# Sources with several edges exchange first-layer sums by a packed list, the other rows stay in edge order, and the relational tiles run in one part

## The reference

```
L0: norm = rsqrt(1 + outdeg); agg[src] = sum of (norm*h)[dst]; x += norm * (agg + norm*h)
L1: w = -dis[src]*dis[dst]; four times feat[src] += sum of w*feat[dst]; x += polynomial(theta) of feat
L2: per edge: msg = sum_b w_comp[type, b] * (h[src] @ weight[b])
    a = tanh(relu(<h[src] A1, h[dst] A2 + rel_emb[type]> / sqrt(32)))
    x[dst] += relu(sum of a*msg over its edges + h[src of its last edge] @ self_loop)
L3: ten times h[dst] = 0.9 * norm * sum of (norm*h)[src] + 0.1 * h0;  x += h
```

## Time and profile before

| | us |
|---|---|
| median of 3 runs | 2677.03 (2675.88 to 2682.1) |
| profiled execution, span | 2683.2 |
| DVE busy | 1746.0 (65%) |
| POOL busy | 1681.8 (63%) |
| PE busy | 434.8 (16%) |
| ACT busy | 341.4 (13%) |
| DMA moved | 84.14 MB, mean 31 GB/s |

### The profile page before, as it was taken

The page is one execution under the profiler, slowest core; times in us unless marked ns, Lnnn a source line. Parts: engine busy times, 40 slices in busy tenths (PEclk is TensorE's granted clock), DMA queues, the critical chain, the costliest instruction groups (busy, mean ns, idle before and its releaser), DMA issues.

```text
span 2683.2 us, 12436 instructions
## 1 busy us (share of the span) xinstructions
PE 434.8 (16%) x2105; PEld 213.7 (8%) x2105; DVE 1746.0 (65%) x2979; ACT 341.4 (13%) x1043; POOL 1681.8 (63%) x1682
## 2 busy tenths in 40 slices
PE   0000000000002000000000069494186000016000
PEld 0000000000001000000000023131132000016000
DVE  8998987987317997619898458887878941321000
ACT  0000012111000021001111034242043110000000
POOL 6566677777753257267777755246456477466776
PEclk9999999999998555555555555555555555555555
DMA  1001022221000033111221100000000120000000
GB/s 21 15 10 26 11 65 52 51 60 41 12 9 5 14 116 128 38 26 52 69 52 50 61 9 10 5 7 8 5 7 7 62 64 10 30 11 10 8 8 8
DMA packets 64970, 84.14 MB, mean 31 GB/s; under 512 B 30264, under 2 KB 57576, under 8 KB 63896
## 3 DMA queue, kind: packets, MB, share of 16 engines
q0 software_dynamic: 53056, 24.10, 6.6%
q1 hardware_dynamic: 6008, 34.00, 3.2%
q10 hardware_dynamic: 5856, 25.60, 2.5%
HBM read 36.45 MB, written 50.96 MB: 33 GB/s over the span
## 4 chain that ended last, share of the span: by engine, by line
issue 43%; DVE 34%; POOL 9%; PE 8%; another core or an unknown queue 4%; DMA 1%; ACT 1%; DVEq 1%; ACTq 0%; POOLq 0%
POOL out L1589 6%; DVE mf L533 5%; DVE pay L533 2%; PE psum L2048 2%; DVE z L533 2%; PE psum L2049 2%; POOL mf L1583 1%; DVE st L1062 1%; DVE outs L533 1%; DVE psum L533 1%; DVE psum L562 1%; DVE z L982 1%; DVE xs L533 1%; DVE z L1393 1%
## 5 line engine op out<-in xcount | busy, mean ns | idle before, releaser
L1583 POOL DMA_INDIRECT mf<-x_rows,i_srcX x196 | 197.8, 1009 | 149.3 <-DVE z L1393 106.7
L1583 POOL DMA_INDIRECT xs<-in_x,i_src x196 | 200.1, 1021 | 142.2 <-issue 58.5
L1589 POOL DMA_INDIRECT out<-outs,i_outS x196 | 198.1, 1011 | 144.5 <-DVE z L1393 80.6
L1583 POOL DMA_INDIRECT xd<-in_x,i_dst x196 | 205.4, 1048 | 109.8 <-DVE mf L533 49.0
L1589 POOL DMA_INDIRECT out<-outs,i_srcX x196 | 196.1, 1001 | 69.2 <-issue 58.9
L1583 POOL DMA_INDIRECT pay<-payload_by_dst,i_rank x196 | 195.2, 996 | 62.8 <-issue 62.8
L533 DVE TENSOR_TENSOR mf<-mf 128x128 f32<-128x128 f32 (+5 forms) x578 | 176.0, 342 | 10.5
L533 DVE TENSOR_TENSOR pay<-psum,pay 128x512 f32<-128x512 f32 x196 | 132.3, 687 | 72.2 <-ACT pay L1926 62.0
L1583 POOL DMA_INDIRECT mf<-l_own_rows,lists x92 | 91.8, 998 | 91.5 <-DMA l_own_rows<-pay 64.1
L2048 PE MATMUL psum<-pay 64*128 64x512 f16 x196 | 117.5, 599 | 106.5 <-ACT pay L1911 77.6
L1393 DVE TENSOR_REDUCE z<-pay 128x512 f32 (+1 forms) x196 | 132.4, 675 | 0.0
(11 more groups left out here) (466 smaller groups left out, 2450.4 us busy)
## 6 DMA issues: line engine op xcount, KB each, us to landing
z<-in_x ACTq DMA_DIRECT2D x14, 624.0 KB
out<-z ACTq DMA_DIRECT2D x14, 624.0 KB
l_first_rows<-mf SPq DMA_DIRECT2D x2, 3234.0 KB
outs<-in_x ACTq DMA_DIRECT2D x6, 624.0 KB
out<-outs ACTq DMA_DIRECT2D x6, 624.0 KB
l_own_rows<-pay SPq DMA_DIRECT2D x1, 3626.0 KB, 10.0
payload_by_dst<-z SPq DMA_DIRECT2D x1, 3234.0 KB
x_rows<-z SPq DMA_DIRECT2D x1, 3234.0 KB
```

What stands on the lines that cost most here:

```text
L1583: G.indirect_dma_start(out=dest(k), out_offset=None, in_=table, in_offset=bass.IndirectOffsetOnAxis(ap=idx[:, k:k + 1], axis=0), bounds_ch ...
L1589: G.indirect_dma_start(out=table, out_offset=bass.IndirectOffsetOnAxis(ap=idx[:, k:k + 1], axis=0), in_=source(k), in_offset=None, bounds_ ...
```

## The change

1. **Rows of sources stay in edge order.** `xs` is gathered by the raw source of each edge (`icols["outS"]`), which needs no sort, 84 + 20 + 92 rows without pace. The third sort now yields, for each edge, whether its source has several edges ("many"), the lead edge of that source, and the pointer for layer 3.
2. **Layer-0 sums by a packed list.** `chosen_edges` and `packed_up` make a list of the edges of sources with several (MANY: room XW0 = 80 a partition, ten rounds for each of two values, five groups, W0 = 46 columns). Only their payload is gathered (46 DMAs), `segment_totals` sums forward and backward over 46 columns x 34 values, and 46 scatters put the totals to `sums_by_edge` in edge order, from which one plain DMA reloads all of `z`.
3. **Layer-1 list in two pieces.** SINGLE (edges of sources with one edge; room 80, ten rounds for each of two values, five groups, WS = 38 columns) and MULTI (those of the packed list that receive, WM = 12), together W1 = 50. FOLLOWING (WF = 12) lists the edges that copy the row of their lead edge behind layer 1: 12 gathers and 12 scatters more.
4. **Dense halves**: three early, two in the middle, two beside the rounds, three behind.
5. **Layer 2 in one part.** x rows come back by one plain DMA (`outs<-x_rows`) and 196 gathers fall away; the layer-3 listing stands ahead of the inputs; inputs of all 196 columns at once; 49 turns in one stretch; sends paced by `l2_done`, SENDS_AHEAD = 12 ahead.

The core of the diff:

```diff
 XW, W = 64, 46
+XW0, W0 = 80, 46
+WS, WM, WF = 38, 12, 12
+W1 = WS + WM
...
-L2_PARTS = ((0, 76), (76, 140), (140, EC))
-XS_PARTS = ((0, 66), (66, 140), (140, 180), (180, EC))
-L2_TURNS = ((0, 18), (18, 34), (34, EC // 4))
+XS_PARTS = ((0, 104), (104, 150), (150, EC))
+ROWS_BEFORE_LIST = 84
+SENDS_AHEAD = 12
...
-MIDDLE_HALF, ROUNDS_HALF, LATE_HALF, HALVES = 2 * EARLY, 2 * EARLY + 1, 2 * EARLY + 3, 2 * TURNS
+MIDDLE_HALF, ROUNDS_HALF, LATE_HALF, HALVES = 3, 5, 7, 2 * TURNS
...
+            values, _, base0 = chosen_edges(act0, (col("cont"), col("head")), XW0, W0)
+            packed_up(values, base0, XW0, W0, MANY, ids0, c["tmp"])
...
+            values, place1, base1 = chosen_edges(act1, (col("dptr"), lin), XW0, WS)
...
+            packed_up(values, base1, XW0, WS, SINGLE, ids1, c["tmp"])
...
+            dve.wait_ge(s["m0_in"], 16 * W0)
...
+            segment_totals(link, W0, M0, Z0, T0, (cont0, next0, end0, head0, tail0), s["totals_in"], s["totals_out"], 1)
...
+            tt(T0i[:, :, D], counti, sloti, ALU.bitwise_or).then_inc(s["sums_ready"], 1)
...
+            spread(place0, receives, (ptr0, lead0, given0), W0, WM, MULTI)
...
+            spread(place0, follows, (lead0, given0), W0, WF, FOLLOWING)
...
+            def chosen_edges(act, given, room, wo):
...
+                for value, out in zip(given, values):
...
+                    for r in range(room // 8):
+                        link(V.max(out=vals[:, 8 * r:8 * r + 8], in_=full))
+                        link(V.match_replace(out=full, in_to_replace=vals[:, 8 * r:8 * r + 8], in_values=full,
+                                             imm_value=0.0))
...
-            pointers(0)
-            l2_inputs(0)
+            dve.wait_ge(s["x2_in"], 16)
...
+            layernorm(OUT, xy[:, :, D:2 * D], Z)
...
+            dve.wait_ge(s["y_table"], 32)
+            layernorm(XD, Z, xy[:, :, D:2 * D])
...
-            l2_turns(*L2_TURNS[0])
-            pointers(1)
-            l2_inputs(1)
-            l2_turns(*L2_TURNS[1])
-            pointers(2)
-            marks["ends"] = link.n
-            link(V.tensor_copy(icols["l3"][:], col("kn")))
-            compact_edges((col("kn"), col("own")), (pf0, owni), wt, EDGES["l3"], c["tmp"])
-            marks["ended"] = link.n
-            l2_inputs(2)
-            l2_turns(*L2_TURNS[2])
+            l2_turns(0, EC // 4)
...
+            source_rows(0, ROWS_BEFORE_LIST)
             pool.wait_ge(s["pay_stored"], 16)
-            gather(lambda k: PAY[:, k, :], pay_dram, icols["edgeS"], last[P * EC], s["payload_in"])
-            for part in range(1, len(XS_PARTS)):
-                source_rows(part)
+            pool.wait_ge(s["many_listed"], 2)
+            gather(lambda q: M0[:, q, 0:PAYLOAD], pay_dram, edge0, last[P * EC], s["m0_in"], W0)
+            source_rows(ROWS_BEFORE_LIST, XS_PARTS[0][1])
+            pool.wait_ge(s["agg_stored"], 16)
+            pool.wait_ge(s["sums_ready"], 1)
+            scatter(agg_dram, lambda q: T0[:, q, 0:PAYLOAD], edge0, last[P * EC], s["sums_scattered"], W0)
+            source_rows(XS_PARTS[0][1], EC)
...
+            for k in range(EC):
+                if k >= SENDS_AHEAD:
+                    pool.wait_ge(s["l2_done"], 2 + k - SENDS_AHEAD)
+                scatter(out, lambda q: OUT[:, q, :], icols["sent"], last[N], s["outs_scattered"], 1, k)
```

More of the change, by code:

```diff
@@ L865, in _ @@
[L865 to L867 removed]
+            word, low = SCRI[1][:, 0:SC], SCRI[2][:, 0:SC]
+            edge, pos, late = (SCR[k][:, 0:SC] for k in (5, 6, 7))
+            state, held = (SCR[k][:, 0:SC] for k in (0, 3))
+            link(ts(word, sortedi, 32767, None, ALU.bitwise_and))
+            link(V.tensor_copy(edge, word))
+            dve.wait_ge(s["low_ready"], 1)
@@ new lines, in packed_up, with pointers @@
+            def packed_up(values, base, room, wo, layout, ids, both):
+                place, valid = c["sq_in"][:, 0:room], chosen[:, 0:room]
+                link(ts(place, iota_p[:, 1:room + 1], base, None, ALU.add))
+                link(tt(place, place, valid, ALU.mult))
+                spread(place, valid, values, room, wo, layout)
+                gathered_up(ids, wo, len(values), both)
+            def pointers(ids, empty, outs):
+                link(ts(empty, ids, 0.5, FAR, ALU.is_lt, ALU.mult))
+                link.many([V.scalar_tensor_tensor(out=out, in0=ids[:, :, k], scalar=-1.0, in1=empty[:, :, k], op0=ALU.add, op1=ALU.add)
+                           for k, out in outs])
@@ new lines, in _ @@
+            V.memset(kept[:, 0:W0 * TOTW], 0.0).then_inc(s["many_listed"], 1)
+            link(ts(valid0, edge_p, 0.5, None, ALU.is_gt))
+            segment_flags(lead_p, W0, cont0, next0, end0, head0, tail0, link)
+            ask(lead_p[:, 0:1])
+            link(V.scalar_tensor_tensor(out=wcarry[:], in0=MISC, scalar=lead_p[:, W0 - 1:W0], in1=upper[:],
+                                        op0=ALU.is_equal, op1=ALU.mult))
+            ask(small[:, 0:1])
+            link(V.tensor_copy(wb0, MISC))
@@ L946, in turn_half @@
                 dense_pair([2 * h, 2 * h + 1], P, DCH, chain, lambda l, b: 12 * i + (3 + 6 * h + 2 * l + b + 1), place)
[L948 to L952, removed]
-                    assert ch.n == PER, ch.n
-                dve.wait_ge(s["dense_done"], UNROLL * last + 1)
             def dense_half(n, place):
@@ new lines, in _ @@
+            link(V.memset(kept[:, 0:kept_w], 0.0))
+            V.memset(kept_keys, FAR).then_inc(s["l1_zero"], 1)
+            dve.wait_ge(s["sums_in"], 16)
+            dve.wait_ge(s["dense_out"], 16 * (2 * MIDDLE_HALF + 1))
+            count, code, inti = col("tmp"), col("tmp2"), c["sq_in"][:].bitcast(i32)[:, 0:EC]
+            link(ts(inti, X2Ti[:, :, D], 15, None, ALU.logical_shift_right))
+            link(V.tensor_copy(count, inti))
+            link(V.scalar_tensor_tensor(out=count, in0=count, scalar=-1.0, in1=col("many"), op0=ALU.add, op1=ALU.mult))
@@ L1625, in _ @@
                 gather(lambda k: XD[:, k, :], x, icols["dst"], last[N], s["xdst_in"], 1, k)
-            pool.wait_ge(s["srows_idx"], 1)
-            def source_rows(part):
-                lo, hi = XS_PARTS[part]
-                for k in range(lo, hi):
-                    behind = k - XS_PARTS[1][0] - ROWS_AT_ONCE
-                    if behind >= 0:
-                        pool.wait_ge(s["dve"], min(marks["listing"] + 5 * behind // 2, marks["summed"]))
-                    gather(lambda k: XS[:, k, :], x, icols["srcS"], last[N], s[f"xsrc_in{part}"], 1, k)
```

1270 lines of the change are left out of this document (700 added, 570 removed).

## The result

The changed kernel is slower: 2780.22 us (median of 4 runs, 2756.01 to 2785.05) against 2679.57 (4 runs of the kernel before, 2675.88 to 2689.07), a ratio of 1.0353 (95% interval 1.031 to 1.0396). The profiled execution has a span of 2777.3 us, 94.1 over the one before. The forecast was 2640.

The account below looks back on a forecast made before the run. DVE was taken to bound until 1073 us, slow instruction links the edge choice, a DVE-ACT-TensorE ring layer 2. Terms -7 + 25 + 8 - 64 = -38 on 2683.2 gave 2645, stated as 2640 us, range 2605 to 2695.

Parts of the forecast that it names:

- The slow links in the new lists: Many and single lists: DVE's short instructions slowed beside POOL's stream, taken as +25 us, 12 for each list.
- the upper bound of 140: Slow-link cost if slow wherever POOL streams: many list +42, single +49, MULTI and FOLLOWING +50, together +140 us.
- the nearest row: Layer-3 listing, same code beside a stream begun at its start: 10 us of slow links for 16 rounds.
- rival 1: New lists, 40 rounds between 405 and 560: slow links cost 60 to 140 us; at 100, 2715 us; chance 0.17.
- "+50" for MULTI and FOLLOWING: Part of the slow-link upper bound: these two lists beside 46 scatters and 92 gathers, +50 us.
- The rest of the sum: Other terms up to the fifth dense half's end: 233 us off, 226 on, so -7 us.
- compact_listed ... +8: Behind the fifth half: compact_listed with 50 columns and a second base, +8 us; rounds and late halves the same.
- Layer 2, "-64": Layer 2: y rows in time -28, listing -9, weight halves -7, inputs -15, turns -8, reload +3: -64 us.
- The tail, counted as the same: Last window behind layer 2, 2061 to 2683: left alone by the change, the same 622 us.
- Rival 2: First part: POOL held by DVE's group building, rows and sums 15 to 20 us late, 2657 us; chance 0.11.
- Rival 3: Layer-2 turns: TensorE's clock rises to full, turn 5.8 us, 66 us less, 2574 us; chance 0.04.
- Rival 4: No change: early stage costs what layer 2 saves, through slow links or two 20 us waits; 2677 us; chance 0.10.

Follow-up runs that it names:

- experiment 10: The kernel of experiment 4 once more, with five rounds: 2592.99 us (six runs), ratio 0.9714 to the kernel before.
- Experiment 2: Changed kernel with POOL's last 92 source-row gathers held until the FOLLOWING list is placed: 2634.19 us, ratio 0.9888 to the kernel before.
- experiment 3: Changed kernel with the last 92 source-row gathers and the 46 scatters of the sums held until the FOLLOWING place: 2625.23 us, one run.
- experiment 4: Changed kernel, 66 instead of 84 rows ahead of the many list, all other source rows and the sums' scatters held until the FOLLOWING place: 2600.74 us, ratio 0.968.
- experiment 7: Kernel before the change, its last 130 source rows held until the listing's first group is made, then unpaced: 2633.1 us, ratio 0.9837.
- experiment 8: Kernel of experiment 4 with 72 rows first and half of the first layer-1 scatters held until the rounds are over: 2624.32 us, ratio 0.979.
- experiment 6: Kernel before the change, without the pacing of its source rows by DVE's count: 2721.67 us, one run.

## Why the prediction was wrong

**The step that failed** is "**The slow links in the new lists**". I took +25 us and gave as the nearest row; the trace has about +170: many list 98 us where 75 were counted, single list 101 (68), MULTI 36 (26; its place took 16.29 us where a free one takes 3), FOLLOWING 129 (24). Against experiment 10, where the stream is kept away, it is 20, 33, 17 and 107, together 177. It is beyond the upper bound of 140 too. Two things were wrong in it. First, the bound counted DVE's instructions only. TensorE's are held up in the same way, and a packed place of 46 columns is 92 of them in a row. I had seen the step on DVE and did not ask which other engine has a long row of short instructions beside the stream. Second, the row that I took as nearest was the lucky one: there the stream had just begun, and DVE ran 90 instructions in 29 us (1846.3 to 1875.5) before the first slow link, 69 more than one per 1.40 us. The new lists begin 80 us into a stream (many) or 41 us into one (single), and what counts is what was used since. From 323.5 to 360.3 DVE ran 104 short instructions beside the changed kernel's gathers, 78 more than one per 1.40 us, with no slow link; then 15 long ones of a LayerNorm in 43 us; and 20 instructions later, at 409.7, the many list was slow. The evidence for the high value was in the earlier trace rows, and rival 1 was that mechanism; it had 0.17 and a price of 100, and most of its true price (105 of 171) sits in a place (FOLLOWING) that it did not name.

**"+50" for MULTI and FOLLOWING beside 46 scatters and 92 gathers** was thus the right place and too small: 13 + 103 us of waits for the places and some 10 us of slow links.

**The rest of the sum held.** Without the slow links the early stage is as counted: in experiment 10 the lists took 78 and 67.6 us (75 and 68), MULTI and FOLLOWING 41 (50), the three early halves in the changed kernel 46.4 each (47.5), the wait for three stores 19.43 (17.8), the sort's decode +9 (+8), totals and codes 29 (32).

**"compact_listed ... +8"**: 27 us more from the fifth half to the last one. The list itself has the 8; the other 20 are slow links again, 11 of the last 32 scans one in 1.40 us and a carry 8.94 us late, beside the 25 scatters. The kernel before has none there. Experiment 2 has none either (193 us), experiments 3 and 4 have them (216), and experiment 10, the same kernel as 4, has half of them (209): the same code falls on one side or the other.

**Layer 2, "-64"**: -86. Right in each mechanism, mis-sized in two. The weight halves, inputs and the start of the turns took 92.5 us (1719.8 to 1812.3) where 147.5 had been spent, the wait of 27.76 that is gone among them; the start took only 4 us where I put 22, and the turns 351 (350). The tail, counted as the same, is 8 us shorter.

**Sum**, by the spans: +161.5 to the fifth half's end (18 forecast), +27 (8), -86 (-64), -8 (0) are +94.5, and the spans differ by 94.1.

**Rival 2** (POOL late) did not happen: rows and sums were in before their norms even with everything held, but for 5.82 us in experiment 4. I had also misread its row: the 9.42 us of POOL ahead of 840.89 are the kernel's own pacing, a wait for DVE's count, and not the lock that rival 2 took it for. In experiment 7, without that pacing, the gathers keep their period of 1.30 us beside the same products:

```profile
741.08 2.28 DVE L533 TENSOR_TENSOR outs<-iota_p,psum 128x2048 f16<-128x2048 f32 x1
742.27 1.00 POOL L1583 DMA_INDIRECT xs<-in_x,i_src  x1 [0.30 <-issue]
743.28 0.91 DVE L533 TENSOR_TENSOR outs<-iota_p,psum 128x736 f16<-128x736 f32 x1
743.57 1.00 POOL L1583 DMA_INDIRECT xs<-in_x,i_src  x1 [0.30 <-issue]
```

**Rival 3** fell in a way that I had not thought of: in several runs the clock was granted at 1.00 in layer 2 and the turns took as long (below). **Rival 4** was wrong about the waits for the totals' gathers: there are none.

**What the change is worth by itself** is not settled. With rows held back in both kernels, it is 2593 to 2601 us against 2633 (experiments 4, 10 and 7; by the ratios to before 0.968 to 0.971 against 0.984), 1.3 to 1.6%. But experiment 7 still has a place of 22.49 us beside its stream, and its tail took 620.2 us against 599.7 and 590.6, in code that the change leaves alone: of the 29 and 57 us between its profiled span and theirs, 20 and 30 lie there. In the form given, the change is 3.5% slower, and with the missing waits put in it is 2.9 to 3.2% faster than before.

**What stays open.** That the step comes with back-to-back transfers of POOL, that it goes by instructions and not by rows, that a gap of 1.5 us lifts it, and that it reaches DVE and TensorE, is shown. Through what it acts is not. The fetch of instructions by DMA is out. The page of the changed kernel counts these packets in its whole span (queue, kind, packets, MB):

```profile
q14 instruction: 46, 0.38, 0.0%
q8 instruction: 5, 0.08, 0.0%
```

They have 8 or 16 KB each, and by the trace none of them starts between 724.0 and 857.7 us, around the wait of 103 us, nor between 378.4 and 469.8, around the slow rounds of the many list. So the instructions were there, and something else let them through one by one; semaphores and the writing of records are candidates that no run here tells apart. Every run of this case was recorded, so what the step costs without the writing of records is not shown. The rule that I cited (the Trainium skill, "Runtime: NRT & Kernel Launch", Instruction fetch mechanics: sequential fetch is mostly hidden) is borne out in this by the trace; my reading of it, that straight code then has no slow links, is not, by 170 us. What decides the lucky or unlucky side in the rounds and in the tail (each 20 us) is open too, but it is the same step: behind the last turn DVE makes 34 to 40 such steps of 1.40 us where the tail takes 614 to 623 us (before, after, experiments 7 and 8) and 15 to 19 where it takes 591 to 600 (experiments 2, 4 and 10).

## What to carry to other kernels

Where a loop of GpSimd transfers has no wait in it, count what the other engines issue beside it, TensorE's matmuls included. Here 69 to 78 of DVE's were free beyond one per 1.40 us near the start of a stream, but only 14 to 18 of TensorE's in a place 30 us behind another one; each one more cost 1.4 us, however short it was. Before gathers that carried a pacing are replaced, look for what the pacing protected; put the stream beside few long instructions (LayerNorms, dense chunks), and hold it, or space it, beside lists, scans and one-hot matmuls. This change removed 256 of 1658 transfers and lost 3.5%; holding 138 of the others back (experiment 3) turned that into a gain.

## What was not expected of the hardware

- The records of TensorE run ahead of its work: the last placing matmul stands at 745.42 us, and its semaphore released DVE at 832.93. A short record is no proof that the engine was done.
- A step of 1.40 us an instruction, in straight code, with no instruction packet on the way: beside POOL's back-to-back transfers it holds up TensorE as well as DVE, and it ends some 7 to 18 us behind the last one (7 in the many list of the changed kernel, 18 in experiment 6).
- The granted clock said nothing of the matmuls' length here. In the kernel of experiment 10 it is 1.00 (2.4 GHz) through layer 2 and in the changed kernel 0.50 (1.2 GHz), with the same busy time. Experiment 10:

```profile
1470.00:1980.00 510.00, 342.77 (x1641) 135.91 (x1641) 427.08 (x717) 170.80 (x841) 200.46 (x196) 1.00 0.02 5
```

  342.77 against 343.89 us for TensorE, and 599 against 600 ns for one 64x512 product. The ends of matmuls are modelled in these records; but the 49 turns, which DVE's own records time, took 349.1 and 349.2 us, so at either level the turn was the same.
